# The prologue of a fused MoE / mixing / MoE kernel: first routing from centered rows, packed loads, copies in halves

## The chip, the cores and the metric

The kernel runs on one core of a Trainium2 chip. The metric is device time in microseconds (us), the median of several executions; for the kernel before it is 808.44 us (three runs, 808.37 to 808.47). Profiles are of one execution each. An engine is one of TensorE (PE; its weight loads are listed as PEld), VectorE (DVE), ScalarE (ACT), GpSimd (POOL) and SyncE (SP, which here only issues DMAs).

## The reference

The input x is 8 sequences of 512 rows of 128 floats. All arithmetic is float32.

```
ffn(z)  = silu(z @ Ws_up) @ Ws_down + sum_e cw[:, e] * (silu(z @ W_up[e]) @ W_down[e])
          64 experts with 64 hidden columns each; cw: affinity z @ centroids.T, plus a bias to
          choose the best 8, sigmoid of the chosen affinities, divided by their sum
attn(z) = y, with xf = z @ WB.T and xb = z @ WBf.T (first/last row kept),
          g = sigmoid(xf.w1 + xb.w2 + b), y = g * (xf + xb) + (1 - g) * z
x = x + 0.5 * ffn(layernorm(x))
x = x + attn(layernorm(x))
x = x + 0.5 * ffn(layernorm(x))
```

All experts are computed for all rows; cw is zero where an expert was not chosen. Layernorm is (x - mean) * rstd, with rstd = (var + 1e-5) ** -0.5.

## The kernel before, in words

The work is 16 phases, two `ffn` passes for each of the 8 sequences. One phase is 33 tiles: tile 0 is the shared expert, tiles 1 to 32 are two experts each. For each tile TensorE makes an "up" product (`up_product`, into one of five PSUM banks `up[t % 5]`) and, six slots later, a "down" product (`down_product`, summed in `y_ps`). Every product is three float32 matmuls of 128x512 on operands split into a high and a low part (`x_hi`, `x_lo`, `wu_hi`, `wu_lo` and so on). Between up and down ScalarE applies SiLU (`silu`), VectorE multiplies by the routing weights (`gate`, needs `cw`), ScalarE makes the high part `g_hi` (`high_part`), and VectorE (even tiles) or GpSimd (odd tiles) the low part `g_lo` (`low_part`). TensorE may overwrite a bank only when the tile five earlier has been gated (`free_bank`).

Each engine runs its own instruction list in the order of the slots of a phase. Tables such as `AT_FIRST` say in which slot a side job stands on each engine: splitting a further eighth of the weights (`wu_hi`, `wu_lo`, `wd_hi`, `wd_lo`; eight `split_up` and eight `split_down` in phase 0), the statistics and the normalising of the next sequence (`stat0`, `aggr0`, `rstd0`, `norm0`; `norm` is L586), its transpose (`x_t`, slot 15 on TensorE), its routing (`aff` to `cw_copy`). Engines wait for each other on semaphores only. In phase 0 `late` is 3: TensorE makes the up products of tiles 0 to 3 before it turns the routing weights (`turn_cw`), and ScalarE does the SiLU of tiles 0 to 3 before `cw_copy`.

Ahead of phase 0 stands the prologue, about 16 us long until the first gate. In order: SyncE issues x, seven small loads, pieces 0 and 1 of both weights (0.5 MB each), then waits for `norm_done[0]` before it reloads `x_in`; eight more small loads stand among the rest. VectorE clears constants and, when x lands, takes mean and variance (`stat`, `aggr`, L573 and L580). GpSimd makes rstd (`rstd_of`, L349), then `sm_lo`. VectorE normalises (L586), TensorE transposes two halves (L922), ScalarE copies them to `x_raw` (L551, L553), TensorE makes the affinities (L791) from `x_raw`, VectorE makes `x_hi`, `x_lo` (L743, L745) and then the routing: `add_bias` L595, `find_top` L601, `take_top` L608, `select` L615 (needs ScalarE's `sig`), `sum_up` L620, `invert` L624, the spread to `w_dup` L753, then one weight split (L659) and the low part of tile 0 (L649). TensorE turns `w_dup` (L781), ScalarE copies it to `cw[0]` (L442), and the first gate (L635) can run. Beside it ScalarE splits the first two eighths of w_up (L537) and GpSimd makes their low parts (L369); up products 1 to 4 wait for the first of these. TensorE fills its waits with matmuls on zeros or on weights whose result is not used (`keep_busy`, L768): 12 at the start, 3 ahead of the affinities, 3 ahead of `turn_cw`.

## Time and profile before

| | us |
|---|---|
| median of 3 runs | 808.44 |
| the profiled execution | 808.82 |
| span of its instructions | 806.9 |
| TensorE busy | 796.3 |
| VectorE busy | 659.6 |
| ScalarE busy | 627.3 |
| GpSimd busy | 424.3 |

The span runs from the first to the last instruction; the profiled execution's own time is 1.9 us longer. All times inside a trace are counted from the span's start. A busy TensorE is one that has a matmul in flight: matmuls overlap, and a 128x512 one starts 0.23 us after the one before and lasts 0.39 us in the records. "Idle before, releaser" names the instruction that let an engine go on.

### The profile page before, as it was taken

How to read it: one execution, taken by the hardware profiler on the slowest of the kernel's cores; microseconds unless marked ns; L12 is line 12 of the kernel's file. 1: busy time of each engine (PE TensorE's matmuls, PEld its weight loads, DVE VectorE, ACT ScalarE, POOL GpSimd, SP SyncE). 2: the span in 40 equal slices, each digit the busy share in tenths (PEclk: the TensorE clock that was granted, in tenths of full speed). 3: DMA queues.
4: the chain of work that ended last, by engine and by line, in shares of the span. 5: the costliest groups of instructions: out<-in, count | busy, mean ns of one | idle time of the engine just before them, and what ended most of it. 6: DMA issues, size and time to landing. Idle time of an engine off the chain costs nothing.

```text
span 806.9 us, 12441 instructions
## 1 busy us (share of the span) xinstructions
PE 796.3 (99%) x3671; PEld 648.4 (80%) x3671; DVE 659.6 (82%) x1426; ACT 627.3 (78%) x1207; POOL 424.3 (53%) x378
## 2 busy tenths in 40 slices
PE   7999999999999999999999999999999999999998
PEld 5787878888888888888888888888888888888786
DVE  6887989779797788977879779797898788787875
ACT  5987777778877778868787678787788787786885
POOL 3885546454555554545545455464554545454453
PEclk9999999999999999999999999999999999999999
DMA  7100000000000000000000000000000000000000
GB/s 258 33 1 13 14 1 1 0 20 8 14 1 0 26 0 13 0 0 26 0 13 0 0 26 0 13 0 0 26 0 0 0 2 27 0 1 1 14 0 14
DMA packets 15901, 11.44 MB, mean 14 GB/s; under 512 B 1664, under 2 KB 14848, under 8 KB 15872
## 3 DMA queue, kind: packets, MB, share of 16 engines
q1 hardware_dynamic: 15872, 11.08, 4.4%
q8 instruction: 15, 0.25, 0.1%
q14 instruction: 14, 0.11, 0.0%
HBM read 8.98 MB, written 2.10 MB: 14 GB/s over the span
## 4 chain that ended last, share of the span: by engine, by line
PE 92%; DVE 3%; ACT 2%; POOL 2%; DMA 1%; SPq 0%; issue 0%; DVEq 0%
PE y_ps L772 14%; PE y_ps L774 14%; PE up L773 14%; PE up L772 14%; PE up L774 14%; PE y_ps L773 14%; PE side L781 3%; PE side L791 2%; PE side L813 1%; PE side L812 1%; POOL g_lo L362 1%; ACT g_hi L481 1%; ACT up L447 1%; DMA wu_raw<-in_w_up 1%; DVE gated L635 0%; DVE g_lo L644 0%
## 5 line engine op out<-in xcount | busy, mean ns | idle before, releaser
L362 POOL TENSOR_TENSOR g_lo<-gated,g_hi 128x512 fp32r<-128x512 f32 x256 | 333.6, 1303 | 339.9 <-ACT g_hi L481 339.1
L447 ACT ACTIVATE up<-up 128x512 f32<-128x512 f32 x513 | 300.2, 585 | 87.4 <-PE up L774 85.4
L635 DVE TENSOR_TENSOR gated<-up,cw 128x512 f32<-128x512 f32 x256 | 175.3, 685 | 85.0 <-ACT up L447 80.2
L772 PE MATMUL y_ps<-g_hi,wd_hi 128*128 128x512 f32 x512 | 207.5, 405 | 1.0 <-POOL g_lo L362 0.9
L772 PE MATMUL up<-x_hi,wu_hi 128*128 128x512 f32 x512 | 202.4, 395 | 0.8 <-POOL wu_lo L369 0.7
L773 PE MATMUL up<-x_lo,wu_hi 128*128 128x512 f32 x512 | 202.5, 396 | 0.0
L774 PE MATMUL y_ps<-g_hi,wd_lo 128*128 128x512 f32 x512 | 202.5, 396 | 0.0
L774 PE MATMUL up<-x_hi,wu_lo 128*128 128x512 f32 x512 | 201.8, 394 | 0.0
L773 PE MATMUL y_ps<-g_lo,wd_hi 128*128 128x512 f32 x512 | 201.5, 393 | 0.0
L635 DVE TENSOR_TENSOR up<-up,cw 128x512 f32<-128x512 f32 x256 | 176.5, 689 | 23.8 <-ACT up L447 18.7
L481 ACT CAST g_hi<-up 128x512 fp32r<-128x512 f32 x256 | 151.1, 590 | 45.5 <-DVE up L635 42.4
L644 DVE TENSOR_TENSOR g_lo<-up,g_hi 128x512 fp32r<-128x512 f32 x256 | 174.4, 681 | 12.2 <-ACT g_hi L481 11.0
L481 ACT CAST g_hi<-gated 128x512 fp32r<-128x512 f32 x256 | 156.5, 611 | 18.5 <-DVE gated L635 18.0
L772 PEld LDWEIGHTS up<-x_hi,wu_hi 128*128 128x128 f32 x512 | 96.4, 188 | 24.0 <-POOL wu_lo L369 1.6
L773 PEld LDWEIGHTS up<-x_lo,wu_hi 128*128 128x128 f32 x512 | 96.4, 188 | 23.0
L774 PEld LDWEIGHTS y_ps<-g_hi,wd_lo 128*128 128x128 f32 x512 | 96.3, 188 | 23.0
L772 PEld LDWEIGHTS y_ps<-g_hi,wd_hi 128*128 128x128 f32 x512 | 96.4, 188 | 22.7 <-POOL g_lo L362 1.2
L774 PEld LDWEIGHTS up<-x_hi,wu_lo 128*128 128x128 f32 x512 | 96.3, 188 | 22.4
L773 PEld LDWEIGHTS y_ps<-g_lo,wd_hi 128*128 128x128 f32 x512 | 96.5, 189 | 19.5
L586 DVE TENSOR_SCALAR normed<-x,mv,rstd 128x128 f32<-128x128 f32 x64 | 29.0, 504 | 1.2 <-POOL rstd L349 1.2
L349 POOL TENSOR_TENSOR rstd<-var_eps,neg_half 128x4 f32<-128x4 f32 x24 | 24.9, 1038 | 2.0
L586 DVE TENSOR_SCALAR normed<-x_in,mv,rstd 128x128 f32<-128x128 f32 x32 | 21.1, 700 | 1.6 <-POOL rstd L349 1.6
(114 smaller groups left out, 504.3 us busy)
## 6 DMA issues: line engine op xcount, KB each, us to landing
x_in<-in_x SPq DMA_DIRECT2D x8, 256.0 KB, 2.8
wu_raw<-in_w_up SPq DMA_DIRECT2D x4, 512.0 KB, 6.2
wd_raw<-in_w_down SPq DMA_DIRECT2D x4, 512.0 KB, 7.0
x_res<-in_x SPq DMA_DIRECT2D x8, 256.0 KB, 2.7
out<-out_sb SPq DMA_DIRECT2D x7, 256.0 KB, 2.2
out<-out_sb SPq DMA_DIRECT2D x2, 128.0 KB, 1.8
ident<-in_ident SPq DMA_DIRECT2D x1, 64.0 KB, 2.4
sm_raw<-in_ws_up SPq DMA_DIRECT2D x2, 32.0 KB, 2.3
```

Source lines behind the costliest of these rows:

```text
L349: nc.gpsimd.tensor_tensor(rstd[k][:, :], var_eps[k][:, :], neg_half[:, :], ALU.pow).then_inc(rstd_done[k], 1)
L362: nc.gpsimd.tensor_tensor(g_lo[:, i, :], gated[:, t // 2 % ORING, :], g_hi[:, i, :].bitcast(fp32), ALU.subtract).then_inc(lo_done[1], 1)
L447: nc.scalar.activation(up[i][:, :], up[i][:, :], ACT.Silu).then_inc(silu_done, 1)
L481: nc.scalar.copy(g_hi[:, t % GRING, :], src).then_inc(hi_done, 1)
L586: made = nc.vector.tensor_scalar(normed[k][:, n, :], norm_from[k][:, n, :], mv[k][:, n, 0:1], rstd[k][:, n:n + 1], ALU.subtract, ALU.mult)
L635: nc.vector.tensor_tensor(gated[:, t // 2 % ORING, :] if t % 2 else up[i][:, :], up[i][:, :], cw[ph.q][:, :], ALU.mult).then_inc(gate_done, 1)
L644: nc.vector.tensor_tensor(g_lo[:, i, :], up[t % RING][:, :], g_hi[:, i, :].bitcast(fp32), ALU.subtract).then_inc(lo_done[0], 1)
L772: nc.tensor.matmul(o, a[0], b[0], start=start, stop=False)
L773: nc.tensor.matmul(o, a[0], b[1], start=False, stop=False)
L774: return nc.tensor.matmul(o, a[1], b[0], start=False, stop=stop)
L781: last = nc.tensor.transpose(rows(dst, n), src(n), ident[:, :])
L791: last = nc.tensor.matmul(aff[:, m, :], rows(x_raw, m), ce_raw[:, :], start=True, stop=True)
```

## The change

Only what stands ahead of and at the start of phase 0 changes; the other 15 phases run the same instructions.

- The layernorm of the first sequence is split: VectorE makes the negated mean, ScalarE adds it to x (`normed[0]`, centered but not scaled, no rstd needed), and TensorE transposes that in halves into `up[2]`, `up[3]`. VectorE copies the halves to `x_raw`, and affinities are made from them, a half at a time. rstd is applied to the affinities instead: in four instructions of VectorE that add the bias too, and as the scale of four Tanh instructions of ScalarE.
- For the up products ScalarE scales the centered rows by rstd into `normed[1]` (four instructions), TensorE transposes these into `up[4]`, ScalarE makes `x_hi`, and VectorE makes `x_lo` after `take_top`, ahead of `select`. The first up product does its two matmuls on `x_hi` before it waits for `x_lo`.
- The small operands come packed on the host in three loads: `route` (identity, centroids, bias), `shared` (shared expert), `mix` (all for attn). Behind x SyncE issues `route`, `shared` and then pieces 0 and 1 of the weights; the eight other small loads become `mix`, and the wait for `consts_set` goes.
- GpSimd, not ScalarE, makes the high part of the first two eighths of w_up, each ahead of its low part.
- The spread to `w_dup`, its transposes and the copies to `cw[0]` go in halves, into two PSUM banks. `late` is 2 on TensorE and 1 on ScalarE: ScalarE does the SiLU of tiles 2 and 3 after the copies.
- The unused matmuls are 11 at the start, begun after two of the memsets instead of all, 1 behind the transposes, and none ahead of `turn_cw`.

The diff, cut to its core:

```
@@ constants, slot table of phase 0 @@
-WARM_START, WARM_ROWS, WARM_ROUTE = 12, 3, 3
+WARM_START, WARM_ROWS = 11, 1
...
-    "late": 3,
+    "late": 2, "late_act": 1,
...
@@ SyncE @@
-            sp.dma_start(ce_raw[:, :], cent_t).then_inc(small_in[0], 16)
-            sp.dma_start(ident[:, :], ident_in).then_inc(small_in[0], 16)
-            sp.dma_start(bias_b[:, :], ebias.partition_broadcast(P)).then_inc(small_in[0], 16)
-            for h in range(2):
-                sp.dma_start(sm_raw[:, SU + h * F:SU + (h + 1) * F], ws_up).then_inc(small_in[1], 16)
-                sp.dma_start(sm_raw[h * F:(h + 1) * F, SD:SD + D], ws_down).then_inc(small_in[1], 16)
+            sp.dma_start(route[:, :], route_dram).then_inc(route_in, 16)
+            sp.dma_start(sm_raw[:, :], shared_dram).then_inc(shared_in, 16)
             load_pieces(0)
             load_pieces(1)
             load_x(1)
-            sp.dma_start(wb_sb[:, :], wb).then_inc(small_in[2], 16)
-            sp.dma_start(wbf_sb[:, :], wbf).then_inc(small_in[2], 16)
-            sp.dma_start(b_col[:, :], b_in.partition_broadcast(P)).then_inc(small_in[2], 16)
-            sp.wait_ge(consts_set, 1)
-            sp.dma_start(sm_raw[:, I1 + D:I1 + D + 1], w1).then_inc(small_in[2], 16)
-            sp.dma_start(sm_raw[:, I2 + D:I2 + D + 1], w2).then_inc(small_in[2], 16)
+            sp.dma_start(mix[:, :], mix_dram).then_inc(mix_in, 16)
             load_pieces(2)
...
@@ GpSimd @@
+            nc.gpsimd.tensor_tensor(sm_lo[:, :], sm_raw[:, :], sm_hi[:, :].bitcast(fp32), ALU.subtract).then_inc(sm_lo_done, 1)
+            for i in range(2):
+                js = slice(i * JS, (i + 1) * JS)
+                pool.wait_ge(wu_in[0], 16)
+                nc.gpsimd.tensor_copy(wu_hi[:, js, :], wu_raw[:, js, :]).then_inc(first_hi_done, 1)
+                split_up(i)
...
@@ ScalarE: start of a phase that has `late` @@
-                    for t in range(ph.late + 1):
+                    for t in range(ph.late_act + 1):
                         up_steps(ph, t)
-                    cw_copy(ph.q, ph.use)
+                    if ph.first:
+                        act.wait_ge(first_cw_half, 1)
+                        nc.scalar.copy(cw[0][:, half(0, T)], side0[:, half(0, T)])
+                        act.wait_ge(cw_turned[0], 1)
+                        nc.scalar.copy(cw[0][:, half(1, T)], side1[:, half(1, T)]).then_inc(cw_done[0], 1)
+                    else:
+                        cw_copy(ph.q, ph.use)
...
@@ ScalarE: ahead of phase 0 @@
-            act.wait_ge(small_in[1], 64)
-            nc.scalar.copy(sm_hi[:, :], sm_raw[:, 0:A1]).then_inc(sm_hi_done, 1)
-            act.wait_ge(half_turned, 1)
-            nc.scalar.copy(x_raw[:, half(0, T)], side0[:, half(0, T)])
+            act.wait_ge(shared_in, 16)
+            nc.scalar.copy(sm_hi[:, :], sm_raw[:, :]).then_inc(sm_hi_done, 1)
+
+            act.wait_ge(neg_mean_done, 1)
+            for m in range(NB):
+                made = nc.scalar.activation(normed[0][:, m, :], x_in[:, m, :], ACT.Identity, bias=neg_mean[:, m:m + 1])
+                if m == NB // 2 - 1:
+                    made.then_inc(half_normed, 1)
+            made.then_inc(norm_done[0], 1)
+            act.wait_ge(norm_done[0], 1)
+            act.wait_ge(rstd_done[0], 1)
+            for m in range(NB):
+                made = nc.scalar.activation(normed[1][:, m, :], normed[0][:, m, :], ACT.Copy, scale=rstd[0][:, m:m + 1])
+            made.then_inc(first_scaled, 1)
             act.wait_ge(x_turned[0], 1)
-            nc.scalar.copy(x_raw[:, half(1, T)], side1[:, half(1, T)]).then_inc(x_copied[0], 1)
-            split_up(0)
-            split_up(1)
+            nc.scalar.copy(x_hi[0][:, :], up[RING - 1][:, :]).then_inc(x_hi_done[0], 1)
+            act.wait_ge(bias_done[0], 1)
+            act.wait_ge(half_rstd_done, 1)
+            for m in range(NB):
+                made = nc.scalar.activation(sig[:, m, :], aff[:, m, :], ACT.Tanh, scale=half_rstd[:, m:m + 1])
+            made.then_inc(half_tanh_done[0], 1)
+            act.wait_ge(half_tanh_done[0], 1)
+            nc.scalar.activation(sig[:, :, :], sig[:, :, :], ACT.Copy, bias=1.0).then_inc(sig_done[0], 1)
             split_down(0)
-            sigmoid(0, 0)
...
@@ VectorE: ahead of phase 0 @@
-            nc.vector.memset(sm_raw[:, I1:I1 + AW], 0.0)
-            nc.vector.memset(sm_raw[:, I2 + D:I2 + AW], 0.0)
+            nc.vector.memset(g_hi[:, 0, :].bitcast(fp32), 0.0)
+            nc.vector.memset(zeros_r[:, :].bitcast(fp32), 0.0).then_inc(zeros_set, 1)
             nc.vector.memset(u_mid[:, 0:1], 0.0)
             nc.vector.memset(u_mid[:, T:T + 2], 0.0)
-            nc.vector.memset(g_hi[:, 0, :].bitcast(fp32), 0.0)
-            nc.vector.memset(zeros_r[:, :].bitcast(fp32), 0.0)
             for edge in (e0, e1):
-                last = nc.vector.memset(edge[:, :], 0.0)
-            last = nc.vector.memset(su_high[:, F:P].bitcast(fp32), 0.0)
-            last.then_inc(consts_set, 1)
+                nc.vector.memset(edge[:, :], 0.0)
+            nc.vector.memset(w_sel[:, :, E:E + 1], SUM_EPS)
+            nc.vector.memset(su_high[:, F:P].bitcast(fp32), 0.0).then_inc(consts_set, 1)
             stat(0, 0)
             aggr(0, 0)
-            nc.vector.memset(w_sel[:, :, E:E + 1], SUM_EPS)
-            norm(0, 0, range(0, NB // 2), False, half_normed)
-            norm(0, 0, range(NB // 2, NB))
-            dve.wait_ge(x_copied[0], 1)
-            nc.vector.tensor_copy(x_hi[0][:, :], x_raw[:, :]).then_inc(x_hi_done[0], 1)
-            dve.wait_ge(x_hi_done[0], 1)
-            nc.vector.tensor_tensor(x_lo[0][:, :], x_raw[:, :], x_hi[0][:, :].bitcast(fp32), ALU.subtract).then_inc(x_lo_done[0], 1)
-            add_bias(0, 0)
+            dve.wait_ge(mv_done[0], 1)
+            nc.vector.tensor_scalar_mul(neg_mean[:, :], mv[0][:, :, 0], -1.0).then_inc(neg_mean_done, 1)
+            for h in range(2):
+                dve.wait_ge(half_turned, h + 1)
+                nc.vector.tensor_copy(x_raw[:, half(h, T)], up[2 + h][:, half(h, T)]).then_inc((half_copied, x_copied[0])[h], 1)
+            dve.wait_ge(rstd_done[0], 1)
+            nc.vector.tensor_scalar_mul(half_rstd[:, :], rstd[0][:, :], 0.5).then_inc(half_rstd_done, 1)
+            dve.wait_ge(aff_done[0], 1)
+            for m in range(NB):
+                made = nc.vector.scalar_tensor_tensor(biased[:, m, :], aff[:, m, :], rstd[0][:, m:m + 1], bias_b[:, :],
+                                                      ALU.mult, ALU.add)
+            made.then_inc(bias_done[0], 1)
             find_top(0, 0)
             take_top(0, 0)
+            dve.wait_ge(x_hi_done[0], 1)
+            nc.vector.tensor_tensor(x_lo[0][:, :], up[RING - 1][:, :], x_hi[0][:, :].bitcast(fp32), ALU.subtract).then_inc(x_lo_done[0], 1)
             select(0, 0)
             sum_up(0, 0)
             invert(0, 0)
             dve.wait_ge(inv_done[0], 1)
-            nc.vector.tensor_tensor(*spread_operands, ALU.mult).then_inc(first_dup_done, 1)
+            for h in range(2):
+                nc.vector.tensor_tensor(*(o[:, half(h, NB), :, :] for o in spread_operands), ALU.mult).then_inc(first_dup_done, 1)
...
@@ TensorE @@
                 if first:
-                    pe.wait_ge(first_dup_done, 1)
+                    for h in range(2):
+                        pe.wait_ge(first_dup_done, h + 1)
+                        for m in range(h * NB // 2, (h + 1) * NB // 2):
+                            last = nc.tensor.transpose(rows((side0, side1)[h], m), block(m), ident[:, :])
+                        last.then_inc((first_cw_half, cw_turned[0])[h], 1)
...
+                if ph.first and t == 0:
+
+                    w = small(SU, SU + P)
+                    nc.tensor.matmul(o[:, :], w[0], x_hi[q][:, :], start=True, stop=False)
+                    nc.tensor.matmul(o[:, :], w[1], x_hi[q][:, :], start=False, stop=False)
+                    pe.wait_ge(x_lo_done[q], 1)
+                    nc.tensor.matmul(o[:, :], w[0], x_lo[q][:, :], start=False, stop=True).then_inc(up_done, 1)
...
                     if ph.late == t:
-                        if ph.first:
-                            keep_busy(WARM_ROUTE, side0, wu_hi[:, 0, :], wu_hi[:, 0:NB, :])
...
+            pe.wait_ge(zeros_set, 1)
+            keep_busy(WARM_START, y_ps[:, :], zeros_r[:, :], g_hi[:, 0, :])
             pe.wait_ge(consts_set, 1)
-            keep_busy(WARM_START, y_ps[:, :], zeros_r[:, :], g_hi[:, 0, :])
-            pe.wait_ge(small_in[0], 48)
+            pe.wait_ge(route_in, 16)
             for h in range(2):
 
                 if h == 0:
@@ -919,10 +958,15 @@
                 else:
                     pe.wait_ge(norm_done[0], 1)
                 for m in range(h * NB // 2, (h + 1) * NB // 2):
-                    last = nc.tensor.transpose(rows((side0, side1)[h], m), normed[0][:, m, :], ident[:, :])
-                last.then_inc(half_turned if h == 0 else x_turned[0], 1)
+                    last = nc.tensor.transpose(rows(up[2 + h], m), normed[0][:, m, :], ident[:, :])
+                last.then_inc(half_turned, 1)
+            pe.wait_ge(half_copied, 1)
+            affinity_blocks(range(0, NB // 2))
+            pe.wait_ge(x_copied[0], 1)
+            affinity_blocks(range(NB // 2, NB)).then_inc(aff_done[0], 1)
+            pe.wait_ge(first_scaled, 1)
+            turn(up[RING - 1], lambda m: normed[1][:, m, :]).then_inc(x_turned[0], 1)
             keep_busy(WARM_ROWS, y_ps[:, :], zeros_r[:, :], g_hi[:, 0, :])
-            affinities(0, 0)
...
```

## Rows read from the trace of the kernel before

**Rows 1.** The page: span, busy time of each engine, TensorE's granted clock in tenths.
```profile
span 806.9 us, 12441 instructions
...
PE 796.3 (99%) x3671; PEld 648.4 (80%) x3671; DVE 659.6 (82%) x1426; ACT 627.3 (78%) x1207; POOL 424.3 (53%) x378
...
PEclk9999999999999999999999999999999999999999
```
**Rows 2.** Windows: length, busy PE, PEld, DVE, ACT, POOL (instructions), clock, DMA share, GB/s.
```profile
0.00:34.15 34.15, 27.89 (x116) 20.62 (x116) 26.62 (x75) 24.02 (x49) 19.00 (x22) 1.00 0.49 164
34.15:800.00 765.85, 765.12 (x3542) 625.74 (x3543) 631.49 (x1349) 602.27 (x1157) 404.39 (x356) 1.00 0.02 7
```
**Rows 3.** Who waited for whom, TensorE: us in total, times, longest.
```profile
PE side L781 <- DVE normed L586: 1.7, 1, 1.7
...
PE up L772 <- POOL wu_lo L369: 0.7, 1, 0.7
```
**Rows 4.** The chain of waits, 0 to 36 us: start, us, what.
```profile
4.92 4.92 DMA wu_raw<-in_w_up
...
15.50 0.60 ACT cw L442
...
16.85 0.62 ACT g_hi L481
...
20.15 0.15 ACT su_high L485
...
23.50 0.49 ACT up L447
...
34.15 0.66 PE side L781 x4
```
**Rows 5.** Timeline of VectorE until the first gate: start, us, line, operation.
```profile
1.54 0.17 DVE L732 MEMSET zeros_r<- 128x128 f32 x1
...
4.51 0.38 DVE L580 BATCH_NORM_AGGREGATE mv<-stats 128x2 f32<-128x6 f32 x4
...
9.38 0.69 DVE L745 TENSOR_TENSOR x_lo<-x_raw,x_hi 128x512 fp32r<-128x512 f32 x1
...
10.08 0.42 DVE L595 TENSOR_TENSOR biased<-side,bias_b 128x256 f32<-128x256 f32 x1
...
10.54 0.61 DVE L601 MAX8 top<-biased 128x8 f32<-128x64 f32 x4
...
11.84 0.21 DVE L608 MATCH_REPLACE8 taken<-top,biased 128x64 f32<-128x64 f32 x1
...
12.45 0.90 DVE L615 SCALAR_TENSOR_TENSOR w_sel<-taken,sig 128x256 f32<-128x256 f32 x1 [0.41 <-ACT sig L438]
...
16.12 0.69 DVE L635 TENSOR_TENSOR gated<-up,cw 128x512 f32<-128x512 f32 x1
```
**Rows 6.** Timeline of TensorE: the first unused matmuls, the affinities.
```profile
2.11 4.66 PE L768 MATMUL y_ps<-g_hi,zeros_r 128*128 128x512 f32 x12 [2.11 <-DVE su_high L735]
...
9.02 1.03 PE L791 MATMUL side<-ce_raw,x_raw 128*128 128x64 f32 x8
```
**Rows 7.** Groups by line and shape: busy us, mean ns, idle before.
```profile
L353 POOL CAST x_hi<-x_raw 128x512 fp32r<-128x512 f32 x15 | 9.2, 612 | 0.0
...
L484 ACT CAST su_both<-sm_hi 128x64 fp32r<-128x64 f32 x1 | 0.2, 240 | 0.0
```
**Rows 8.** VectorE's lines 615 (whole run) and 586 (30 to 35 us): ns min/median/max.
```profile
L615 DVE SCALAR_TENSOR_TENSOR w_sel<-taken,sig x16: 425/918/1069, 12.5 to 751.4; 128x256 f32<-128x256 f32 x16
...
L586 DVE TENSOR_SCALAR normed<-x_in,mv,rstd x4: 333/664/1328, 30.7 to 33.8; 128x128 f32<-128x128 f32 x4
```
**Rows 9.** POOL's first two wu_lo, and SyncE's first w_up piece.
```profile
4.92 0.59 SPq L300 DMA_DIRECT2D wu_raw<-in_w_up  x1
...
10.55 2.53 POOL L369 TENSOR_TENSOR wu_lo<-wu_raw,wu_hi 128x512 fp32r<-128x512 f32 x2 [2.91 <-ACT wu_hi L537]
```
**Rows 10.** The four w_up loads (line 300), from issue to landing.
```profile
DMA to landing us min/median/max: 4.9/6.2/6.8
```

More of the change, by code:

```diff
@@ L50, in __init__ @@
         self.p, self.q, self.at, self.first, self.late = p, q, at, first, at.get("late")
+        self.late_act = at.get("late_act", self.late)
         self.use = p // 2 if isinstance(p, int) else use
@@ L129, in over_phases, with build @@
     phase(Phase(2 * c + 1, 1, AT_LAST, post=c - 1, keep=c))
[L132 removed]
+def build(nc, x, route_dram, shared_dram, mix_dram, w_up, w_down, out):
     fp32, fp32r = mybir.dt.float32, mybir.dt.float32r
@@ L507, in phase @@
                 for t in range(SLOTS):
-                    if t < NT and (ph.late is None or t > ph.late):
+                    if t < NT and (ph.late is None or t > ph.late_act):
                         up_steps(ph, t)
@@ L948, with column @@
     w_down = np.asarray(L0_ffn_W_down).reshape(E, NJ, R, D).transpose(0, 2, 1, 3).reshape(P, NJ, D)
[L949 to L954 removed]
+    def column(a):
+        return np.stack([np.asarray(a).reshape(D), np.zeros(D, np.float32)], axis=1)
+    eye, none = np.eye(P, dtype=np.float32), np.zeros((P, 2), np.float32)
+    ws_up, ws_down = np.asarray(L0_ffn_Ws_up), np.asarray(L0_ffn_Ws_down)
+    route = lay(np.concatenate([eye, np.asarray(L0_ffn_centroids).T, np.tile(np.asarray(L0_ffn_expert_biases), (P, 1))], axis=1))
+    shared = lay(np.concatenate([ws_up, ws_up, np.concatenate([ws_down, ws_down])], axis=1))
+    mix = lay(np.concatenate([WB, WBf, WB.T, none, WBf.T, none, np.zeros((P, D), np.float32), column(L0_attn_w1),
+                              eye, column(L0_attn_w2), np.tile(np.asarray(L0_attn_b), (P, 2))], axis=1))
+    arrays = {
+        "x": lay(L0_attn_u), "route": route, "shared": shared, "mix": mix, "w_up": lay(w_up), "w_down": lay(w_down),
     }
```

89 lines of the change are left out of this document (43 added, 46 removed).

## Prediction

> **What bounds the kernel now.** I read the page first: TensorE is busy 99% of the span and at full granted clock in every slice, so a change of 0.2% can only come from where TensorE stands idle [rows 1]. The windows say where that is: from 34.15 us to 800 us it is busy 765.12 of 765.85 us, but in the 34.15 us ahead of that it has work for only 27.89 [rows 2]. The table of waits gives the last early gap: 1.7 us in front of the transposes at 34.15 us, waiting for VectorE's `normed` [rows 3]. So whatever moves that moment moves the end by as much, and nothing that only packs TensorE tighter before it does.
>
> The chain of waits tells what sets 34.15. The load of the first w_up piece is on it from 4.92 us, through GpSimd's `wu_lo`, up products and the transposes of `w_dup`, to ScalarE's `cw` copy, which ends at 16.10; the first gate starts at 16.12 [rows 4, 5]. From 16.85 the chain is 14 pieces of ScalarE without a hole, the last from 23.50 to 23.99, and then VectorE, up to the transposes at 34.15 [rows 4]. VectorE's own routing steps end at the same place: it comes free for the first gate at about 16.08. Two paths that tie, so shortening the load alone would give nothing.
>
> **The change, part by part.** I add up the new path to the first gate, in times of the trace.
>
> *Mean to transposes.* `aggr` ends at 4.89 [rows 5]. The negated mean is 4 elements a partition: above 0, under the 0.17 of a 128-column memset; I take 0.15 and get 5.05. The four centering instructions of ScalarE have 128 columns: above 0.15 each (the spacing of 64-column ones) and under 0.60 (512 columns, with its latency) [rows 4, 7]; taken near the short end, 0.22 apart, half are done at 5.6 and all at 6.0. TensorE's 12 unused matmuls ended at 2.11 + 4.66 = 6.77 [rows 6]. They now start at about 1.5 (two memsets and a smaller one leave the front; `zeros_r` ended at 1.71 and two small ones ahead of it go) and are 11, 0.39 less: end 5.9 [rows 5, 6]. So centering is hidden, and the transposes begin at 5.9. Rstd, which used to stand ahead of them, is off this path.
>
> *Transposes to affinities.* Four transposes cost 0.66 [rows 4]; half, with latency, 0.4: 6.3. VectorE's half copies read PSUM, 256 columns, like `biased`, 0.42 [rows 5]: 6.75 and 7.15. The second half of the affinities is half of 1.03 [rows 6]: ready at 7.7, where it was 10.05. This is the gain, 2.35.
>
> *Affinities to `select`.* The bias was one instruction of 0.42; as four of 64 columns it costs at least that and at most 4 x 0.21, the length of a 64-column `MATCH_REPLACE8` [rows 5]. I take 0.6: 8.35. `find_top` 0.64 and `take_top` 0.87, by the starts before: 9.9. Now `x_lo`, 0.69 [rows 5], stands in front of `select`: 10.6. It was done before the routing, so this moves it and saves nothing. `x_hi` isn't late: scaling (after rstd, 6.4) ends at 7.4, the four transposes at 8.4, the ScalarE copy at 0.6 more, 9.0. Sigmoid: four Tanh of 64 columns, 0.15 apart, and 0.42, end near 10.2, so the old wait of 0.41 for `sig` is gone; what is late next is `x_lo` itself.
>
> *The weights.* SyncE issues the first piece after two small loads instead of seven, at (4.92 - 1.24)/7 = 0.53 each: 2.3 instead of 4.92 [rows 9]. Landing 4.9 to 6.8 after issue [rows 10], the short end for the first one: 7.2. Reloads, `mix` and pieces 2 and 3 stand behind SyncE's wait for `norm_done`, now 6.0 instead of 8.0, so none comes later. GpSimd first has `sm_lo` until 7.2, then copy, subtraction, copy, subtraction: 2 x 0.61 + 2 x 1.27 = 3.8 [rows 7, 9], end 11.05. The up products have their first low part at 9.2, early enough; ScalarE loses two copies. But `select` takes 0.425 alone and 0.92 in the median, and beside `wu_lo` (10.55 to 13.08) it took 0.90, ending 0.27 behind GpSimd [rows 5, 8, 9]: it seems to wait for GpSimd's instruction. So it ends at 11.05 + 0.45 = 11.5, not 11.05.
>
> *`select` to the gate.* Before, from 13.35 to 16.12, 2.77. The half split of `w_dup` adds one instruction's overhead, 0.1 (at least 0, at most 0.42 - 0.35 a half, twice): the gate is at 14.35. The other path: `w_dup` half one 12.6, turned and copied, both copies by 13.8, hidden. The 0.9 us of unused matmuls that stood ahead of `turn_cw` were hidden and are worth nothing. The first up product ends at 11.1, tile 2 at 12.5, in time. First gate: 16.12 - 14.35 = 1.75 earlier.
>
> *Behind the gate.* ScalarE is the chain from 16.85 to 23.99. It used to do the SiLU of tiles 2 and 3 while it waited for the transposes. With `late_act` 1, tile 2's fits in the wait for the first gate, but tile 3's falls into the stretch without holes: + 0.49, the spacing of a SiLU there [rows 4]. Left: 1.75 - 0.5 = 1.25 at 24 us, and nothing behind it changes its instructions, so 1.25 at 34.15 and at the end. Profiled execution: 808.82 - 1.25 = 807.6. Profiled time stands 0.4 over the median of the runs: 808.44 - 1.25 = 807.2; I round the gain to 1.3, **807.1**.
>
> **Rivals.**
> *A*, the above. Its uncertain terms are the four-part instructions (0.4), `select` (0.45) and the gate chain; gain 0.7 to 1.9, 806.5 to 807.7. Chance 0.53.
>
> *B, two of the charges don't arise.* If `select` slips in before GpSimd's last subtraction (0.45) and the extra SiLU finds a hole (0.5), the gain is 1.25 + 0.95 = 2.2: 806.2. For it: `select` did run in 0.425 in places [rows 8], and the gain at the affinities is 2.35. Against it: the 14 pieces without a hole. Chance 0.25.
>
> *C, TensorE's clock.* The 12 matmuls took 0.39 each against 0.23 later: something at the start is slow, though the granted clock reads full, 2.4 GHz, even across the gaps [rows 1, 6]. After the change there are fewer unused matmuls (11 + 1 against 18) and a new gap from 9.7 to 10.6. If products then go at the early pace, six of them and the transposes cost 1.0 to 1.2, the `cw` copies end at 14.9 and not 13.8, and the gate comes at 14.95: gain 0.65; with the products behind them slow too, 0.3, 808.1. The Trainium skill (TensorE: Matmul & The Clock Gate, What's actually happening) says that the default is the throttled state, 1.2 GHz, and activity releases it; the trace shows no fall of the granted clock, so by that rule no more than this chance. Chance 0.12.
>
> *D, slower: the weights land late and GpSimd, which now makes high and low parts, holds `select`.* Its work ends at T + 3.8 for a landing at T (if T is over 7.2), `select` 0.45 later, the gate 2.85 later: the gain at 34 us is 16.12 - (T + 7.1) - 0.5 = 8.5 - T. It is zero at T = 8.5, 6.2 after the issue, which is the median landing [rows 10]; at the longest, 6.8, 9.1 and a loss of 0.6 (809.0); over 0.2% lost it is from T = 10.2 (810.1). For it: x, `route`, `shared` and four pieces are now in flight together. Against it: the load of 4.92 us had the same 512 KB ahead of it and the same three pieces beside it. The Trainium skill (SBUF — State Buffer, Who interferes with whom) says that a VectorE instruction with two SBUF inputs and a GpSimd one that reads SBUF exclude each other for a whole instruction; by that rule `select` would wait only for the instruction that runs, so this rival would cost up to 1.3 less. The 1.3 us of [rows 8] in one 128-column `normed`, which needs 0.33, bears the rule out. Chance 0.08, of it half beyond 0.2%.
>
> *E, it doesn't reach the gate:* another wait (`route`, the halves) keeps 16.12 in place: 808.4 to 808.9. Chance 0.02.
>
> **Numbers.** What a measurement of this kernel can tell from no change is about 0.2%, 1.6 us. Faster by more: B and a third of A, 0.42. Within: the rest of A, C, E, half of D, less what I keep for the unforeseen: 0.52. Slower: 0.06. Range: B's end is near 805.9, C's 808.1 and D's loss to 808.6: 805.9 to 808.5.
>
> **What the profile after would show.** `aff` done near 7.7; unused matmuls ending before 6.0; first w_up piece landed by 7.3; `select` starting near 10.6 and lasting over 0.8 beside GpSimd; first gate at 14.35; ScalarE without holes from about 15.1 to 22.7 with one SiLU more; the transposes that wait for `normed` at about 32.9. I am wrong if that last time has not moved by what the first gate moved less 0.5, or if TensorE is idle again behind it; in particular, VectorE's four `normed` (2.8 us instead of 1.3, behind GpSimd's instructions [rows 8]) can fall otherwise by half a microsecond either way.

## Result: slower by 3.1 us, and the profile after

The changed kernel takes **811.55 us** (median of six runs, 810.75 to 812.43) against 808.44: ratio 1.0038, 95% interval 1.0025 to 1.0051. 807.1 was forecast. The profiled execution took 811.56 us, with a span of 809.8. The page answers to [rows 1]:

```profile
span 809.8 us, 12438 instructions
...
PE 797.9 (99%) x3669; PEld 646.7 (80%) x3669; DVE 659.4 (81%) x1427; ACT 629.7 (78%) x1216; POOL 424.5 (52%) x380
...
PEclk9999999999999999999999999999999999999999
```

The span is 2.9 us longer. The prologue isn't where they are. Windows of the changed kernel (columns as in [rows 2]):

```profile
0.00:34.27 34.27, 27.79 (x113) 20.27 (x113) 26.18 (x76) 25.75 (x58) 20.15 (x24) 1.00 0.48 166
...
34.15:800.00 765.85, 765.02 (x3534) 622.88 (x3535) 630.40 (x1348) 601.76 (x1154) 403.11 (x355) 1.00 0.02 7
```

From 34.15 to 800 us TensorE is as busy as before, at the same granted clock, but it has done 3534 matmuls and not 3542 [rows 2]. Each one comes a little later. Over all consecutive 128x512 matmuls between 40 and 795 us whose starts lie under 0.3 us apart, the mean distance of starts in the trace is 232.64 ns before and 233.21 ns after.

The table of waits for TensorE, then the chain from 0 to 36 us:

```profile
PE side L803 <- DVE normed L603: 1.7, 1, 1.7
...
PE up L860 <- DVE x_lo L769: 1.3, 1, 1.3
...
PE up L857 <- ACT x_hi L566: 0.5, 1, 0.5
```
```profile
1.78 4.41 DMA sm_raw<-in_shared
...
6.21 0.36 ACT sm_hi L552
...
6.82 0.98 ACT normed L556 x3
...
8.74 0.93 DVE half_rstd L760
...
15.73 0.70 DVE gated L652
...
17.60 0.48 ACT up L445
...
34.27 0.66 PE side L803 x4
```

The transposes that wait for `normed` are at 34.27, where they were at 34.15 [rows 3, 4], and the first gate is at 15.73 (16.12 in [rows 5]). The chain no longer begins with a piece of w_up but with the packed load `shared`. The steps of the prologue in the timeline:

```profile
1.59 5.06 PE L790 MATMUL y_ps<-g_hi,zeros_r 128*128 128x512 f32 x11 [1.59 <-DVE zeros_r L745]
...
6.21 0.40 ACT L552 CAST sm_hi<-sm_raw 128x256 fp32r<-128x256 f32 x1 [3.98 <-DMA sm_raw<-in_shared]
6.52 1.27 ACT L556 ACTIVATE normed<-x_in,neg_mean 128x128 f32<-128x128 f32 x4
...
7.68 0.61 POOL L418 CAST wu_hi<-wu_raw 128x512 fp32r<-128x512 f32 x1 [0.27 <-DMA wu_raw<-in_w_up]
7.80 0.95 DVE L758 COPY x_raw<-up 128x256 f32<-128x256 f32 x2 [2.61 <-PE up L961]
...
8.28 1.18 PE L812 MATMUL side<-route,x_raw 128*128 128x64 f32 x8
8.37 1.27 POOL L364 TENSOR_TENSOR wu_lo<-wu_raw,wu_hi 128x512 fp32r<-128x512 f32 x1
8.66 1.01 DVE L760 TENSOR_SCALAR half_rstd<-rstd 128x4 f32<-128x4 f32 x1
...
9.59 0.85 DVE L763 SCALAR_TENSOR_TENSOR biased<-side,rstd,route 128x64 f32<-128x64 f32 x4
...
12.49 0.41 DVE L632 SCALAR_TENSOR_TENSOR w_sel<-taken,sig 128x256 f32<-128x256 f32 x1
...
15.73 0.69 DVE L652 TENSOR_TENSOR gated<-up,cw 128x512 f32<-128x512 f32 x1
```

The third part of the loss is at the end. From the start of the last 128x512 matmul to the end of the span it was 4.67 us; it is 5.73 now. So the span's 2.9 us are 0.12 up to the transposes, 1.72 from there to the last 128x512 matmul (769.80 against 768.08), and 1.06 behind it. TensorE's clock didn't fall in this execution; in most of the six it did, as the experiments show.

### The profile page after: what moved, and what is told of

It is laid out like the page before. It is cut to its first block, busy times and chain, and to the rows that moved or that the text cites. A ratio compares the mean times of both kernels' runs of the same rounds, so it can differ in the third digit from the quotient of the medians.

```text
span 809.8 us, 12438 instructions
## 1 busy us (share of the span) xinstructions
PE 797.9 (99%) x3669; PEld 646.7 (80%) x3669; DVE 659.4 (81%) x1427; ACT 629.7 (78%) x1216; POOL 424.5 (52%) x380
## 4 chain that ended last, share of the span: by engine, by line
PE 91%; DVE 4%; ACT 2%; POOL 1%; DMA 1%; issue 0%; SPq 0%; DVEq 0%
PE y_ps L794 14%; PE y_ps L795 14%; PE y_ps L796 14%; PE up L794 14%; PE up L796 14%; PE up L795 14%; PE side L803 3%; PE side L812 2%; PE side L845 1%; PE side L844 1%; POOL g_lo L353 1%; ACT g_hi L479 1%; ACT up L445 1%; DMA sm_raw<-in_shared 1%; DVE gated L652 0%; DVE g_lo L661 0%
## 5 line engine op out<-in xcount | busy, mean ns | idle before, releaser
L346 POOL TENSOR_TENSOR x_lo<-x_raw,x_hi 128x512 fp32r<-128x512 f32 x15 | 19.3, 1289 | 1.2
```

Of the source, the lines that this page charges most:

```text
L346: nc.gpsimd.tensor_tensor(x_lo[q][:, :], x_raw[:, :], x_hi[q][:, :].bitcast(fp32), ALU.subtract).then_inc(x_lo_done[q], 1)
```

## Experiments

All ratios are against the kernel before, run beside each group on the same chip (808.47 to 808.51). "Gate" is the start of the first `gated`, "turn" the start of the transposes behind `normed`, "stream" the time from there to the last 128x512 matmul, "tail" from there to the span's end, all in the profiled execution.

| kernel | gate | turn | spacing, ns | stream | tail | median (range) | ratio, 95% |
|---|---|---|---|---|---|---|---|
| before | 16.12 | 34.15 | 232.64 | 768.08 | 4.67 | 808.44 | |
| after | 15.73 | 34.27 | 233.21 | 769.80 | 5.73 | 811.55 (810.75–812.43) | 1.0038, 1.0025–1.0051 |
| e1 before, 64 B | 15.63 | 33.65 | 233.28 | 769.79 | 4.66 | 810.14 (810.04–810.28) | 1.0020, 1.0011–1.0030 |
| e2 after, 192 B | 15.46 | 34.01 | 232.66 | 768.15 | 5.34 | 809.44 (808.80–810.65) | 1.0013, 1.0004–1.0023 |
| e3 | 15.60 | 34.14 | 233.19 | 769.77 | 5.49 | 810.44 (809.96–811.22) | 1.0025, 1.0015–1.0034 |
| e4 | 14.57 | 33.10 | 233.23 | 769.81 | 5.39 | 810.35 (809.90–811.35) | 1.0025, 1.0014–1.0035 |
| e5 | 15.90 | 34.45 | 232.67 | 768.17 | 5.68 | 809.19 (808.23–811.33) | 1.0011, 1.0001–1.0020 |
| e6 | 15.46 | 34.00 | 232.66 | 768.19 | 5.41 | 808.79 (808.14–809.44) | 1.0002, 0.9992–1.0012 |
| e9 | 14.79 | 33.34 | 232.61 | 768.08 | 5.58 | 808.84 (808.29–809.31) | 1.0004, 0.9995–1.0014 |
| e10 | 14.89 | 32.91 | 232.62 | 768.06 | 5.33 | 808.15 (807.57–808.79) | 0.9995, 0.9985–1.0004 |
| e11 | 15.39 | 33.94 | 232.60 | 768.10 | 4.66 | 808.97 (807.99–809.70) | 1.0006, 0.9997–1.0016 |
| e12 | 15.70 | 33.73 | 232.73 | 768.29 | 5.68 | 809.28 (808.95–809.72) | 1.0010, 1.0001–1.0020 |
| e15 | 16.14 | 34.17 | 232.73 | 768.25 | 4.68 | 808.47 (808.31–809.01) | 0.9999, 0.9990–1.0009 |
| e18 | 14.98 | 33.52 | 232.63 | 768.15 | 4.73 | 808.29 (808.04–809.11) | 0.9999, 0.9989–1.0009 |
| e14 | 14.90 | 32.91 | 232.73 | 768.42 | 4.67 | 807.82 (807.45–808.39) | 0.9990, 0.9981–1.0000 |
| e17 | 15.77 | 33.36 | 232.62 | 768.07 | 4.67 | 807.87 (807.40–808.29) | 0.9991, 0.9981–1.0001 |
| e13 | 14.93 | 32.94 | 232.71 | 768.27 | 4.69 | 807.57 (807.20–807.82) | 0.9988, 0.9978–0.9997 |

### The pace of the stream: where the tiles lie

The change removes some SBUF tiles and adds others. By the sizes in the two programs, every tile allocated from `x_raw` on (`x_hi`, `x_lo`, `g_hi`, `out_sb` and the rest) lies 64 bytes further in each partition; the weights lie where they did. The first pair puts this shift alone into the kernel before, and in the changed one adds 192 bytes to it: the tiles are then 256 bytes from where they were, at the old addresses modulo 256.

```diff
 # e1: before;  e2: after, with [P, 48]
+        pad = sb("pad", [P, 16])
         x_raw = ...
```

> The kernel before, with one unused tile of 64 bytes a partition in front of x_raw, so that every tile behind it lies where the changed kernel has it (64 bytes further; x_hi, x_lo, g_hi, g_lo at 64 instead of 0 modulo 128 and 256). Placement theory: the spacing of back-to-back matmuls goes from 232.6 ns to 233.2 ns, the stretch behind 34 us gets 1.7 us longer, and the last store lands later, so about 810.5 to 811 us. Rival (the stream's pace and the late store come with the changed program or with the execution, not with addresses): 808.4 us, 232.6 ns, transposes behind `normed` at 34.15 us.

> The changed kernel with an unused tile of 192 bytes in front of x_raw, so that x_hi, g_hi, x_in, out_sb and all behind x_raw start at the same value modulo 256 as in the kernel before. Placement theory: spacing back at 232.6 ns, the end 1.7 us (stream) and up to 1.0 us (store) earlier than 811.55: 808.6 to 809.8 us. Rival (not addresses): 811.5 us, 233.2 ns. Either way the transposes behind `normed` stay at 34.27 us.

Windows of e1, then of e2:

```profile
34.15:800.00 765.85, 765.17 (x3535) 622.92 (x3534) 630.22 (x1348) 602.06 (x1154) 403.20 (x355) 1.00 0.02 7
```
```profile
34.15:800.00 765.85, 765.08 (x3542) 625.65 (x3542) 631.40 (x1349) 602.58 (x1157) 404.13 (x356) 1.00 0.02 7
```

The kernel before with a pad that nobody reads does 3535 matmuls in the window and is 1.7 us slower (810.14); the changed kernel with its tiles moved on does 3542 again and gains 2.1, of which 1.65 are in the stream; the rest is tail, prologue and clock, which this edit doesn't aim at. The spacing follows the pad both ways: 233.28 and 232.66 ns. Shown: the placement costs 1.7 us here, and none of it is work; what counts is not how far the tiles move but where they start, since 256 bytes further is as good as not moved (128 wasn't tried). Why 64 bytes matter to TensorE isn't shown. The operands it streams (`x_hi`, `x_lo`, `g_hi`, `g_lo`) are among the moved tiles, but so are VectorE's and GpSimd's, and no run moves one of them alone.

### The prologue: the load `shared` and `half_rstd`

```diff
 # e3, ScalarE (e4 has this too)
-            act.wait_ge(shared_in, 16)
-            nc.scalar.copy(sm_hi[:, :], sm_raw[:, :]).then_inc(sm_hi_done, 1)
             ... four centering activations ...
+            act.wait_ge(shared_in, 16)
+            nc.scalar.copy(sm_hi[:, :], sm_raw[:, :]).then_inc(sm_hi_done, 1)
 # e4, VectorE
             ... neg_mean ...
+            dve.wait_ge(rstd_done[0], 1)
+            nc.vector.tensor_scalar_mul(half_rstd[:, :], rstd[0][:, :], 0.5).then_inc(half_rstd_done, 1)
             ... the two half copies ...
-            dve.wait_ge(rstd_done[0], 1)
-            nc.vector.tensor_scalar_mul(half_rstd[:, :], rstd[0][:, :], 0.5).then_inc(half_rstd_done, 1)
```

> The changed kernel, with ScalarE's sm_hi copy (which waits until 6.2 us for the `shared` load) behind the four centering instructions instead of ahead. If the late load in front of ScalarE is what cost the prologue its gain: centering starts at 5.2 instead of 6.5, the transposes at about 6.65 (end of the unused matmuls) instead of 7.35, the first gate at about 15.0 instead of 15.73, and the transposes behind `normed` at 33.5 instead of 34.27. Rival (another term, such as the half_rstd instruction behind GpSimd, decides): first gate within 0.2 us of 15.73. Time: 811.55 less what the transposes move.

> As the one before, and VectorE's half_rstd (1.01 us behind GpSimd's wu_lo in the changed kernel, needed 0.17) ahead of the two half copies. If it waits for GpSimd's port there, it costs nothing ahead of them and the bias starts right behind the affinities: another 0.5 to 0.9 us off the first gate, transposes behind `normed` at 32.6 to 33.0. Rival: GpSimd's sm_lo holds it in the new place as well, and the half copies start later: no gain over the run before.

e3 gained 0.13 us at the gate in its profile (why is in the next section), though its median is 1.1 us below that of the changed kernel. e4's timeline comes closest to the forecast prologue:

```profile
5.06 1.28 ACT L554 ACTIVATE normed<-x_in,neg_mean 128x128 f32<-128x128 f32 x4 [2.83 <-DVE neg_mean L755]
...
6.39 0.17 DVE L757 TENSOR_SCALAR half_rstd<-rstd 128x4 f32<-128x4 f32 x1 [1.36 <-POOL rstd L340]
...
8.41 0.86 DVE L763 SCALAR_TENSOR_TENSOR biased<-side,rstd,route 128x64 f32<-128x64 f32 x4 [0.87 <-PE side L812]
...
11.33 0.41 DVE L632 SCALAR_TENSOR_TENSOR w_sel<-taken,sig 128x256 f32<-128x256 f32 x1
...
14.57 0.69 DVE L652 TENSOR_TENSOR gated<-up,cw 128x512 f32<-128x512 f32 x1
```

Centering begins at 5.06 instead of 6.52, `half_rstd` takes 0.17 us instead of 1.01, the gate is at 14.57 and the turn at 33.10: 1.17 earlier than in the changed kernel, and the median is 1.2 lower. So the two edits together win back most of what the prologue lacked (1.37), and the rows give nearly all of it to `sm_hi`. In the changed kernel the affinities end at 9.46 (8.28 + 1.18) and the bias starts at 9.59: most of the 1.01 us of `half_rstd` lay beside the affinities, and it held the bias by 0.13 at most. In e3, where `half_rstd`, unmoved but reached earlier, had slipped in ahead of `wu_lo`, the bias starts at 8.37 (row in the next section), in e4 at 8.41. So moving `half_rstd` as well brought the bias no further, which is the rival's outcome, though not by its mechanism: `half_rstd` wasn't held in its new place. The medians agree: e4 is only 0.1 us below e3. One profile doesn't settle tenths here: e1 and e12 have the old prologue, and their turns are at 33.65 and 33.73. What held `half_rstd` is read from the timeline of the changed kernel: it has 4 elements a partition, starts at 8.66 inside GpSimd's `wu_lo` (8.37 to 9.64), and ends with it, at 9.67; in the profiles of e11 and e2 it took 0.89 and 1.27 us and ended 0.03 and 0.02 behind `wu_lo`, and in e2 it held the bias by 0.39 at most. The Trainium skill (SBUF — State Buffer, Who interferes with whom) says that VectorE and GpSimd share one pair of ports as an exclusive lock, taken for a whole instruction, and that `tensor_scalar`, which this is, can take it. By that rule the size of the VectorE instruction doesn't matter, and the trace agrees: 1.01 us beside `wu_lo`, 0.17 alone.

### TensorE's clock

Why e3 gained so little is seen in its windows:

```profile
8.00:10.00 2.00, 1.46 (x10) 1.07 (x9) 1.56 (x10) 1.25 (x6) 1.91 (x3) 1.00 0.96 277
10.00:12.00 2.00, 0.90 (x5) 0.49 (x4) 2.00 (x9) 1.26 (x5) 1.80 (x2) 1.00 1.00 346
12.00:14.00 2.00, 2.00 (x6) 1.51 (x5) 1.90 (x6) 1.49 (x3) 0.00 (x0) 0.50 1.06 414
14.00:16.00 2.00, 2.00 (x9) 1.71 (x8) 1.33 (x3) 1.33 (x4) 0.00 (x0) 0.64 1.02 416
```

After 1.1 us without a matmul behind two lone ones, the granted clock falls to 0.50, the 1.2 GHz level, from 12 us on. The up products then start 0.43 us apart instead of 0.23, and the gate waits 0.64 us for the `cw` copy behind them, in the timeline of e3 (its first rows are those of `half_rstd` before `wu_lo`, and of `select` behind the second `wu_lo`):

```profile
7.54 0.25 DVE L760 TENSOR_SCALAR half_rstd<-rstd 128x4 f32<-128x4 f32 x1
...
8.37 0.86 DVE L763 SCALAR_TENSOR_TENSOR biased<-side,rstd,route 128x64 f32<-128x64 f32 x4 [0.58 <-PE side L812]
...
8.70 1.27 POOL L364 TENSOR_TENSOR wu_lo<-wu_raw,wu_hi 128x512 fp32r<-128x512 f32 x1
...
10.61 1.27 POOL L364 TENSOR_TENSOR wu_lo<-wu_raw,wu_hi 128x512 fp32r<-128x512 f32 x1
...
11.29 0.88 DVE L632 SCALAR_TENSOR_TENSOR w_sel<-taken,sig 128x256 f32<-128x256 f32 x1
...
12.39 0.63 PE L796 MATMUL up<-x_hi,wu_lo 128*128 128x512 f32 x1
12.82 0.63 PE L794 MATMUL up<-x_hi,wu_hi 128*128 128x512 f32 x1
...
15.60 0.69 DVE L652 TENSOR_TENSOR gated<-up,cw 128x512 f32<-128x512 f32 x1 [0.64 <-ACT cw L506]
```

The profiles of e5 and e6 show the same fall; those of the changed kernel, e2, e4, e11 and e14 don't, with nearly the same gaps (the changed kernel is busy 0.84 us of the two from 10 to 12, with three matmuls). Of the 1.03 us by which e3's gate is later than e4's, 0.64 is this wait; the other 0.4 is `select`, which took 0.88 beside GpSimd's second `wu_lo` in e3 (0.41 behind it in e4).

How often the clock fell is on record too, as the mean granted clock of every execution. It is 0.997 in the profiled executions of e3, e5 and e6, and 0.999 or 1.000 in all others that were profiled. Taking 0.998 or less as a fall, it fell in 4 of the changed kernel's 6 executions (medians 811.69 with it, 811.15 without), in 7 of 10 of e3, 5 of e11, 4 of e5, 3 of e2, 2 of e6 and e14, 2 of 9 of e4, 1 of e10 and e12, and in none of the kernel before, e1, e15, e9, e13, e17 and e18. e11 gives the price: its five executions with a fall took 809.27 to 809.70, the five without 807.99 to 808.66, so about 1.0 us for one fall. The mark is coarse: e10's one execution under it took 807.82, less than e10's median.

The Trainium skill (TensorE: Matmul & The Clock Gate, What's actually happening) says that the default is the throttled state and that activity releases it; e3's profile agrees, with 0.50 granted behind the gap and 1.00 again from 16 us.

e6 puts e4, the placement of e2 and the 24 waits of e5 (next section) together; e9 adds six unused matmuls.

```diff
 # e9, e18 (against e6, e11)
-WARM_START, WARM_ROWS = 11, 1
+WARM_START, WARM_ROWS = 11, 3
                 ... first up product, behind its two matmuls on x_hi ...
+                    keep_busy(4, y_ps[:, :], zeros_r[:, :], g_hi[:, 0, :])
                     pe.wait_ge(x_lo_done[q], 1)
```

> As the one before, with sm_hi behind the centering and half_rstd ahead of the half copies too. Sum of the parts, if they add: transposes behind `normed` at 33.1, stream 768.1, tail 4.7: span 805.9, about 807.6 us; with the tail not mended 808.4. In some executions TensorE's clock may fall to 1.2 GHz at about 12 us, as in the profile of the run with sm_hi moved alone (spacing 0.43 us there): then 0.5 to 1 us more, and a spread of over 1 us between runs.

> As e6_all_three, with 3 unused matmuls instead of 1 ahead of x_hi and 4 more ahead of x_lo, in TensorE's two waits of 0.5 and 1.2 us. If the fall of TensorE's clock in some executions makes the spread of the changed kernel (810.75 to 812.43, before 808.37 to 808.47), the runs now agree within 0.4 us and the median is 0.3 to 0.8 under e6_all_three. Rival (the spread comes from the DMAs' landing): same median and spread as e6_all_three.

> e11_place_dve_minus1 (the changed kernel with placement and last fetch mended: 808.97 us, 807.99 to 809.7) with the six extra unused matmuls. By the clock theory the slow executions go and the median comes to 808.2 to 808.6, spread under 0.7. Rival (the changed prologue's spread comes from when its loads land, shared in front of ScalarE above all): still over 1 us apart and 808.9.

e6 missed its number, 808.79 for 807.6: the tail wasn't mended (808.4 was expected then), and in its profile the clock fell and the gate came at 15.46. e9, in which it fell in no execution, moved the gate to 14.79 but not the median (808.84), nor did the spread (1.0 us) shrink to the 0.4 expected. In the two pairs whose tail is whole the same six do gain: e11 808.97 to e18 808.29 (spread 1.7 to 1.1 us, under 0.7 expected), e14 807.82 to e13 807.57 (0.9 to 0.6), a little less than the 0.3 to 1.0 expected. In e13's windows the stretch that was nearly empty is filled, at full clock:

```profile
10.00:12.00 2.00, 1.76 (x8) 1.14 (x7) 2.00 (x9) 1.19 (x4) 1.75 (x2) 1.00 1.03 358
```

So the six matmuls are worth 0.25 to 0.7 us in the median, by how often the clock would have fallen without them (2 and 5 of 10). The difference of 0.25 is no larger than the spread of one kernel's runs. What is left of that spread isn't the clock, since e9 and e18 still spread over 1.0 and 1.1 us; it stays open. The landing of `shared` is a candidate: 2.7 to 4.4 us after its issue in the profiles of the changed kernel and its variants.

### The tail: a last instruction fetch

Where the tail is longer, SyncE's two final stores land 2.2 to 2.4 us after issue, otherwise 1.8 to 1.9. Both kernels have one 8 KB packet of the instruction queue in the last microseconds; the question was what decides whether it meets the store. The suspects were the lengths of the engines' programs. SyncE's (e5) and ScalarE's (e15) were brought to the length that they have in the other kernel; VectorE's, of which the changed kernel has one instruction more, in both directions (e11, e12).

```diff
 # e5: e2, and ahead of SyncE's loop
+            for _ in range(24):
+                sp.wait_ge(route_in, 16)
 # e11: e2, and
-            nc.vector.memset(u_mid[:, 0:1], 0.0)
-            nc.vector.memset(u_mid[:, T:T + 2], 0.0)
+            nc.vector.memset(u_mid[:, :], 0.0)
 # e12: before, and
-            for edge in (e0, e1):
-                last = nc.vector.memset(edge[:, :], 0.0)
+            for edge in (e0[:, 0:64], e0[:, 64:P], e1[:, :]):
+                last = nc.vector.memset(edge, 0.0)
 # e15: before, and ahead of ScalarE's phase 0
+            for k in range(11):
+                nc.scalar.copy(gated[:, 0, 4 * k:4 * k + 4], neg_half[:, :])
```

> The changed kernel with its tiles back at the placement of before (192 unused bytes in front of x_raw) and 24 redundant waits on SyncE ahead of its loop, which bring SyncE's program from 4160 back to 4928 bytes, its size before. In the changed kernel an 8 KB instruction fetch runs through the final store and one DMA engine ends late (last matmul to end of span 5.4 to 5.7 us, before 4.67). If the length of SyncE's program places that fetch, it moves behind the store and the tail is 4.7 us again: about 0.7 us under the run with the placement alone (809.44), 808.7. Rival (another engine's program, or the addresses in HBM, place it): tail still 5.3 or more, 809.4.

> The changed kernel with the placement of before (809.44 us so far) and one VectorE instruction fewer: the two memsets of u_mid's edges become one of the whole tile. VectorE's program is then 54336 bytes, as before, and not 54400. If the end of VectorE's program decides when the last 8 KB instruction fetch comes, it moves from the middle of the final store to behind it: from the last matmul to the end of the span 4.7 us instead of 5.3 to 5.7, about 808.7 us, and runs that lie closer together. Rival (ScalarE's or GpSimd's program decides): tail 5.3 or more, 809.4.

> The kernel before with one VectorE instruction more at the start: the memset of e0 in two halves. By the VectorE theory the last fetch falls into the final store: tail 5.3 to 5.7 instead of 4.67, 809.2 us, runs further apart than 0.2 us. By the rival nothing happens: 808.45.

> The kernel before with 11 small copies on ScalarE (4 elements, while it waits for its first load), so that its program has the 51072 bytes of the changed one instead of 50368. By the ScalarE theory the last fetch falls into the final store: tail 5.3 to 5.7, about 809.2 us, runs further apart. By the VectorE theory the tail stays 4.67 and the time 808.45.

The DMA view from 798 to 812 us (GB/s in 40 slices of 0.35 us; the stores with their median landing). First e11, then e12:

```profile
GB/s 0 0 0 0 0 0 0 0 0 0 0 0 0 0 0 0 0 0 0 75 296 241 138 0 0 0 0 0 23 0 0 0 0 0 0 0 0 0 0 0
...
out<-out_sb SPq DMA_DIRECT2D x2, 128.0 KB, 1.9
```
```profile
GB/s 0 0 0 0 0 0 0 0 0 0 0 0 0 0 0 0 0 0 0 89 284 238 138 9 9 6 0 0 0 0 0 0 0 0 0 0 0 0 0 0
...
out<-out_sb SPq DMA_DIRECT2D x2, 128.0 KB, 2.4
```

The same view of the kernel before, then of the changed one:

```profile
GB/s 0 0 0 0 0 0 0 0 0 0 0 0 0 0 0 0 0 0 0 0 234 198 309 9 0 0 0 0 23 0 0 0 0 0 0 0 0 0 0 0
...
q14 instruction: 1, 0.01, 0.2%
...
out<-out_sb SPq DMA_DIRECT2D x2, 128.0 KB, 1.8
```
```profile
GB/s 0 0 0 0 0 0 0 0 0 0 0 0 0 0 0 0 0 0 0 0 0 0 0 0 0 126 240 285 98 10 10 3 0 0 0 0 0 0 0 0
...
q14 instruction: 1, 0.01, 0.3%
...
out<-out_sb SPq DMA_DIRECT2D x2, 128.0 KB, 2.4
```

With one VectorE instruction less (e11, and before) the stores end, and the fetch stands apart behind them (23 GB/s in its slice). With one more (e12, after) no separate fetch is left, and the store drags a thin end, 6 to 9 GB/s in e12 and 3 to 10 in the changed kernel. The packet's own start says the same: 807.98 in the kernel before and 807.81 in e11, when the stores had ended at 806.14 and 805.95; 805.85 in e12 and 807.55 in the changed kernel, when they ran on until 806.87 and 808.92. The tail is 4.66 in e11 and 5.68 in e12 (e11's median, 808.97 for 808.7 expected, has five falls of the clock in it); by medians one instruction costs the kernel before 0.8 us, and its removal gains e2 0.5 (0.8 if only executions without a fall of the clock are compared, 809.27 to 808.43) and e10 0.6 (e13, which drops e5's waits as well). SyncE's program (tail 5.68) and ScalarE's (4.68) change nothing: the theory behind e5 fell. Shown: the tail goes with VectorE's instruction count, both ways, and with the place of the fetch. That this packet is VectorE's fetch, and that it is what holds the store up, is the likely reading; the record doesn't name an engine, and no run moves the packet by itself.

### The better version, and `late`

e10 gives ScalarE one copy less behind the gate: GpSimd makes high and low part of the third eighth of w_up too. e13 is e10 with one VectorE instruction less and without e5's waits. e14 is e13 without the six unused matmuls, e17 e13 with the old `late`.

```diff
 # e10 (against e9)
-... "wu_hi": (None, None, 2, 5, 8, 12, 16, 20), "wu_lo": (None, None, 5, 7, 11, 15, 19, 23)
+... "wu_hi": (None, None, None, 5, 8, 12, 16, 20), "wu_lo": (None, None, None, 7, 11, 15, 19, 23)
-            for i in range(2):
-                pool.wait_ge(wu_in[0], 16)
+            for i in range(3):
+                pool.wait_ge(wu_in[i // 2], 16)
+                if i == 2:
+                    pool.wait_ge(wd_lo_done[0], 1)
 # e17 (against e13)
-    "late": 2, "late_act": 1,
+    "late": 3, "late_act": 3,
```

> As e9_fillers, and GpSimd makes high and low part of the third eighth of w_up too, in its idle time after VectorE's first wd_lo. ScalarE's stretch without holes behind the first gate loses one copy of 0.52. If that stretch is what sets 34 us (and the SiLU of tile 3 in it cost 0.5 in the changed kernel), the transposes behind `normed` come 0.5 us earlier than in e9_fillers: 32.6. Rival (VectorE or GpSimd bound there): unchanged within 0.1.

> e10_pool_third_eighth without SyncE's redundant waits and with one VectorE instruction fewer. By the VectorE theory: transposes behind `normed` at 32.9, stream 768.1, tail 4.7, span 805.7: 807.4 us, 0.7 under e10_pool_third_eighth, and faster than before by 1.0. By the ScalarE theory: 808.15, its program has 51008 bytes.

> e13_best_dve_minus1 (807.57 us, 807.20 to 807.82) without the six extra unused matmuls: 1 ahead of x_hi and none ahead of x_lo, as in the changed kernel. If TensorE's gaps there let its clock fall in some executions and that price reaches the end, the median is 0.3 to 1.0 us higher and the runs spread over more than 1 us. Rival (the fall is hidden behind VectorE's path, the spread had to do with the final store alone): 807.6 us, spread 0.6.

> e13_best_dve_minus1 with `late` 3 and `late_act` 3 as in the kernel before: the SiLUs of tiles 2 and 3 stand ahead of the cw copies again. If tile 3's SiLU in ScalarE's stretch costs 0.5 us, the way from the first gate to the transposes behind `normed` gets 0.5 shorter (18.0 in e13, so 17.5), while the first gate waits for the fourth up product and comes up to 1.0 later. Rival (the SiLU fits in somewhere): the way stays 18.0 and the time goes up by what the gate loses.

e10: from gate to turn it is 18.02 us instead of 18.55 in e9, one copy of 0.52 (the turn is at 32.91, 0.43 earlier than e9's; 32.6 was expected). e17: 17.59 instead of e13's 18.01, so the old order is 0.42 shorter behind the gate, but the gate, which now waits 0.83 us for the `cw` copy, is 0.84 later; the change's `late` is the better one. e13, **807.57 us**, is the only kernel here whose interval lies below 1 as a whole: 0.9 us less than before. The gate in its timeline:

```profile
14.93 0.69 DVE L655 TENSOR_TENSOR gated<-up,cw 128x512 f32<-128x512 f32 x1
```

## Why the prediction was wrong

The forecast was 4.45 us too low. In the profiled execution 1.4 of these are in the prologue (1.25 forecast as gained, 0.12 lost), 1.7 in the stream and 1.1 in the tail; the rest, 0.3, is within the spread of its runs. Three steps failed: the stretch behind the transposes was taken as unchanged, the first centering had no wait for `shared`, and the clock was counted as not falling.

**Behind the transposes: the step that failed first.** "Nothing behind it changes its instructions, so 1.25 at 34.15 and at the end." The instructions are the same, yet the stretch isn't: +1.72 for the placement (e1, e2) and +1.06 for the fetch (e11, e12). My range contained neither term, because I had taken "same instructions" for "same time". Even with the forecast prologue the kernel is slower: e4 has the turn at 33.10 and takes 810.35.

**Mean to transposes: failed.** I had centering start at 5.05, hidden by the unused matmuls. It started at 6.52. ScalarE's `sm_hi` copy stands ahead of it, and waits for `shared`, which landed at 6.19, 4.41 us after its issue, with four 0.5 MB pieces behind it. I had put no wait there at all. How late `shared` is differs: it landed 2.7 to 4.3 us after its issue in the variants' profiles. Also under-sized were the unused matmuls (they end at 6.65, not 5.9: they start 0.43 us apart to the last, while the last of the 12 before were 0.24 apart), which in e4, with centering early, are what the transposes wait for, and the centering itself (1.27 for 0.9).

**Transposes to affinities:** the copies in halves took 0.95 for 0.85 and the stretch as a whole 2.1 for 1.8 (7.35 to 9.46). About right, once it starts.

**Affinities to `select`: under-sized.** The bias took 0.85 for 0.6. `half_rstd` was in none of my terms: its own work is 0.17 us, it took 1.01 behind `wu_lo`, and of that 0.13 was at most on the path of the bias (0.39 in e2). The rule on `select` and GpSimd that I weighed in rival D was at work, in an instruction that I hadn't listed.

**`select` behind GpSimd:** the charge of 0.45 didn't arise. `select` ran at 12.49 in 0.41 us, since GpSimd was done at 11.56. That part of rival B came true because everything ahead of `select` was late. The mechanism is right where the two meet: in e3 `select` took 0.88 and ended at 12.17, 0.29 behind GpSimd, and in e4 it started at 11.33, just after GpSimd's end at 11.27. The sum also has a slip: 7.2 and 3.76 make 10.96, not 11.05.

**The weights:** right. The first piece was there at 7.6 (forecast 7.2), so rival D fell.

**Behind the gate:** right. ScalarE's chain holds one SiLU more, and the way from gate to turn grew from 18.03 to 18.54 us, 0.51 for the forecast 0.49; taking that SiLU out again (e17) shortens it by 0.42. The turn moved by what the gate moved, less that.

**Rival C: its chance of 0.12 was too small.** Its mechanism is real: the clock fell in 4 of 6 executions, at the gap for `x_lo` (11.5 to 12 us) in the three profiles that show it, and in e3 up products and transposes ran late as it says. I took the trace's lack of a fall as evidence, but that was the trace of a kernel with more unused matmuls ahead of that gap and more work in it (TensorE busy 1.10 of the two us from 10 to 12, against 0.84). The price is about 1 us in an execution with a fall (e11), near C's forecast of 0.6 to 0.95; in the changed kernel's median, which mixes both kinds, it is a few tenths.

With the two prologue waits mended (e4), gate (14.57 for 14.35) and turn (33.10 for 32.9) come within about 0.2 us of the forecast. In part that is luck: `select` starts at 11.33 instead of 10.6, 0.7 late, and ends only 0.24 after the forecast 11.5, because the charge of 0.45 behind GpSimd doesn't arise there. From `select` to the gate the sum is sound: 2.83 us for 2.85.

## To carry to other kernels

When an edit adds or drops SBUF tiles or instructions, compare the pace of a stretch that it doesn't touch (matmuls in a fixed window) and the last few microseconds before looking for the cause in the edited part; a dummy tile or one instruction less tells within two runs. List every instruction of a moved step, even those of four elements, with what stands ahead of it on its in-order engine: a small load behind which the big ones are issued, or a long GpSimd instruction, sets its time, not its size. Then see from the rows how much of that time was on the path before charging it. Where unused matmuls are taken out, look at the granted clock of every execution, not of the profiled one alone.
